# Quantised layers of a decoder block moved beside the next batch's attention, with three batches in progress

## What is computed

```python
def attention(x):                      # qkv = x @ Wqkv.T + b, one k, v of 32 columns
    scores = where(causal, q @ k.T / sqrt(32), min_val)
    return softmax(scores) @ v @ out_w.T + out_b

def smooth_quant_linear(x, w):         # twice a batch: w 512x512, then 512x256
    s = sqrt(max(amax_columns(x), EPS) / max(amax_columns(w), EPS))
    xs, ws = x / s, w * s
    x_scale, w_scale = amax_rows(xs) / 127, amax_rows(ws) / 127
    return round(xs / x_scale) @ round(ws / w_scale).T * x_scale * w_scale.T

def ffn(x):                            # DFF 1376, rank 8, 8 experts, w: top-2 weights
    gate = x @ W_gate + lora(x, sA_gate, sB_gate) + experts(x, A_gate, B_gate, w)
    up = x @ W_up + ...                # the same
    hidden = silu(gate) * up
    return hidden @ W_down + lora(hidden, ...) + experts(hidden, ...)

x = x + attention(layernorm(x))
x = x + linear(silu(gate) * up, ctx_1024)   # gate, up = linear(layernorm(x), fside)
x = x + ffn(layernorm(x))
```

## Time and profile before

| what | us |
|---|---|
| median of three runs | 1168.69 |
| lowest, highest | 1168.50, 1169.06 |
| the profiled execution | 1169.19 |
| its span, first to last instruction | 1167.1 |

### The profile page before, as it was taken

One profiled execution on the slowest core, in us unless ns is written; L12 is line 12 of the kernel. 1 busy time (PEld: TensorE's weight loads), 2 busy tenths in 40 slices (PEclk: granted clock), 3 DMA queues, 4 the chain that ended last, 5 costly groups with the idle time before them and its releaser, 6 DMA issues.

```text
span 1167.1 us, 12967 instructions
## 1 busy us (share of the span) xinstructions
PE 961.7 (82%) x5206; PEld 667.3 (57%) x5214; DVE 595.1 (51%) x801; ACT 314.3 (27%) x484; POOL 242.7 (21%) x177
## 2 busy tenths in 40 slices
PE   2698895446898998878898997878989988859997
PEld 1464353324665566656665576556655666638885
DVE  2254567654444647663644476753544566642222
ACT  2323331432132321432132313232223213311010
POOL 2412333442010214030002113220002121301010
PEclk9757686658899999998998999988999999969999
DMA  7562563526522443225325332444224422244541
GB/s 261 163 221 99 209 243 114 185 123 251 112 106 106 157 145 135 106 105 184 100 92 199 108 119 90 151 154 108 92 91 189 146 92 104 90 153 171 184 172 57
DMA packets 41439, 166.05 MB, mean 142 GB/s; under 512 B 4956, under 2 KB 7772, under 8 KB 32420
## 3 DMA queue, kind: packets, MB, share of 16 engines
q1 hardware_dynamic: 41380, 165.22, 40.8%
HBM read 120.97 MB, written 27.20 MB: 127 GB/s over the span
## 4 chain that ended last, share of the span: by engine, by line
PE 58%; DVE 24%; POOL 7%; issue 5%; ACT 3%; SPq 1%; DMA 1%; POOLq 0%; DVEq 0%; ACTq 0%
PE ring L852 8%; PE ring L853 7%; PE ring L854 7%; PE av L957 4%; DVE negm L1204 4%; PE slot L943 3%; PE den L957 3%; PE slot L923 3%; PE slot L852 3%; PE slot L853 3%; PE slot L854 3%; DVE rden L1224 3%; PE ring L1088 2%; DVE qm L1294 2%; POOL x L650 2%
## 5 line engine op out<-in xcount | busy, mean ns | idle before, releaser
L1204 DVE TENSOR_REDUCE negm<-slot 128x4 f32<-128x512 f32 (+2 forms) x96 | 99.2, 1046 | 128.7 <-PE slot L923 128.3
L852 PE MATMUL ring<-xT_h,gu 128*128 128x512 f32 x352 | 149.1, 423 | 9.8 <-DVE gated L1390 8.8
L655 POOL TENSOR_TENSOR hd_l<-hd,hd_h 128x512 fp32r<-128x512 f32 x44 | 57.4, 1305 | 463.0 <-ACT hd_h L828 463.0
L853 PE MATMUL ring<-xT_l,gu 128*128 128x512 f32 x352 | 140.9, 400 | 0.0
L854 PE MATMUL ring<-xT_h,gu 128*128 128x512 f32 x352 | 140.4, 399 | 0.0
L730 ACT ACTIVATE probs<-slot 128x256 f32<-128x256 f32 (+3 forms) x128 | 86.9, 703 | 130.0 <-PE slot L943 129.1
L852 PEld LDWEIGHTS ring<-xT_h,gu 128*128 128x128 f32 x352 | 68.4, 194 | 36.3 <-DVE gated L1390 17.4
L854 PEld LDWEIGHTS ring<-xT_h,gu 128*128 128x128 f32 x352 | 68.0, 193 | 15.7
L943 PE MATMUL slot<-qst,kst 98*128 98x128 f32 (+3 forms) x256 | 75.6, 388 | 0.0
L853 PEld LDWEIGHTS ring<-xT_l,gu 128*128 128x128 f32 x352 | 68.6, 195 | 9.9
L852 PE MATMUL ring<-dn,hd_h 128*128 128x512 f32 x176 | 74.0, 420 | 0.0
(11 more groups left out here) (194 smaller groups left out, 1741.8 us busy)
## 6 DMA issues: line engine op xcount, KB each, us to landing
gu<-gu_parts SPq DMA_DIRECT2D x44, 1280.0 KB, 5.5
dn<-dn_parts SPq DMA_DIRECT2D x8, 2304.0 KB, 8.6
gu_parts<-gu SPq DMA_DIRECT2D x11, 1280.0 KB, 5.5
qst<-qT_h SPq DMA_DIRECT2D x64, 128.0 KB, 2.4
raw_gu<-gu SPq DMA_DIRECT2D x11, 640.0 KB, 7.6
dn<-dn_parts SPq DMA_DIRECT2D x4, 1728.0 KB, 6.9
dn_parts<-dn SPq DMA_DIRECT2D x11, 576.0 KB, 6.0
x_in<-x SPq DMA_DIRECT2D x4, 1024.0 KB, 7.3
```

Of the source, the lines that this page charges most:

```text
L655: pool.tensor_tensor(hd_l[:, i, :], hd[:, :], hd_h[:, i, :].bitcast(F32), ALU.subtract).then_inc(hd_lo.sem, 1)
L852: pe.matmul(out_, w_hi_, m_hi_, start=start, stop=False, skip_group_check=True)
L853: pe.matmul(out_, w_hi_, m_lo_, start=False, stop=False, skip_group_check=True)
L1204: dve.tensor_reduce(negm[:, h0:h0 + heads, qt].rearrange("p (a c) -> p a c", a=2), slots[SLOT["max", b, g, i]][:, :, 0:heads // 2 * n].rea ...
```

## The change

Three things are done.

- **Order.** The layer has a list of its own, `layer_steps(b)`. `beside` puts it between the steps of the attention of batch b + 1, and `merged` adds the preparation's second half (b = 0) or the feed-forward of batch b - 1. The first half of the preparation stays beside the attention of batch 0. The layer of batch 3 goes with the feed-forward of batch 2; that of batch 3 still stands alone. After a step that claims a slot (`HELD`) the layer's next steps follow at once, until the slot is read.
- **Places.** `xn`, `w_raw`, `d_raw` and `wrow` exist twice: for batch 0 in the region of `xT`, from batch 1 on over the qkv weights. So these are stored once at the start (`wqkv_out`) and fetched once for batch 3 (`wqkv_again`). `hid` lies in `x_in`; `tile_max`, `rows`, `a_bf`, `th` and `x3` have a region of their own. x2 goes through memory (`x2_save`, `x2_copy`). `hd` has as many buffers as `hd_h`, and to make room there are 4 hidden slots for 5, and segments of 3, 3, 3 and 2 tiles.
- **Splits.** The statistics, norms, maxima, scalings, row maxima, the reciprocals of `context`, the bias addition and the layer's weight scaling are each issued in halves or quarters. `gated` is a step two quarters ahead of the product `hd`.

```diff
-SEGMENTS = ((0, 1, 2, 3), (4, 5, 6, 7), (8, 9, 10))
-HID_SLOTS = 5
+SEGMENTS = ((0, 1, 2), (3, 4, 5), (6, 7, 8), (9, 10))
+HID_SLOTS = 4
...
+HELD = MLP_TENANTS + ("colmax", "undo0")
...
+        yield ("turn1", b, s), 0.9, 0.3
+    if b == 0:
+        yield ("x_load", 1), 0, 0
+        yield ("x_again", 0), 0, 0
+        for tt in range(TT):
+            yield ("bias", 0, tt), 0, 0
+    yield ("kv", b), 2.8, 0.3
     for e in range(KT):
-        yield ("q", b, e), 2.2
-    yield ("v", b), 2.5
+        yield ("q", b, e), 2.8, 2.2
...
+        yield ("pause",), 0, 0.7
+        if idx in (1, 2) and g:
+            yield ("split_context", b, g - 1, idx - 1), 0, 0
...
+def layer_steps(b):
+
+
+    for h in range(2):
+        yield ("ln2_stats", b, h), 2
+    yield ("w_load", b), 0
+    for h in range(2):
+        yield ("ln2_norm", b, h), 2
     for n in range(2):
-        if n == 0:
-            yield ("ln2_stats", b), 3
-            yield ("ln2_norm", b), 4
-        else:
+        halves = range(2 - n)
+        if n:
+            yield ("d_load", b), 0
             yield ("tanh", b), 1.5
-            yield ("wmax", b, 1), 1
+        for h in halves:
+            yield ("wmax", b, n, h), 2
+        if n:
             yield ("act", b), 3
-        yield ("xmax", b, n), 3 if n == 0 else 2
-        scale = 1.0 if n == 0 else 0.6
...
+    for h in range(2):
+        yield ("residual", b, h), 2
+    yield ("x2_save", b), 0
+    yield ("x_load", b + 2), 0
+    yield ("wqkv_again", b + 2), 0
+    for h in range(2):
+        yield ("ln3_stats", b, h), 2
+    for h in range(2):
+        yield ("ln3_norm", b, h), 2
+    yield ("x_again", b + 1), 2
+    for h in range(2):
+        yield ("ln1_stats", b + 2, h), 2
+    for h in range(2):
+        yield ("bias", b + 1, 2 * h), 1
+        yield ("bias", b + 1, 2 * h + 1), 1
+        yield ("ln1_norm", b + 2, h), 1
...
+                if name == "up" and k == 1:
+                    yield ("gated", b, f), 0
...
+def beside(attention, layer, first, last):
+
+    attention, layer = list(attention), list(layer)
+    names = [step for step, _, _ in attention]
+    lo, hi = names.index(first) + 1 if first else 0, names.index(last) + 1
+    span, whole = sum(own + room for _, own, room in attention[lo:hi]), sum(w for _, w in layer)
     out, have, used, n = [], 0.0, 0.0, 0
-    for step, r in attention:
+    for i, (step, own, room) in enumerate(attention):
+        out.append((step, room))
+        if lo <= i < hi:
+            have += (own + room) * whole / span
+        while n < len(layer) and (i >= hi or i >= lo and used < have or n and layer[n - 1][0][0] in HELD):
+            used += layer[n][1]
+            out.append((layer[n][0], 0))
+            n += 1
+    return out + [(step, 0) for step, _ in layer[n:]]
+
...
+PREPARATION = list(preparation_steps())
+FIRST_PART = len(PREPARATION) // 2
+ORDER = merged([(step, room) for step, _, room in attention_steps(0)], PREPARATION[:FIRST_PART])
+ORDER += merged(beside(attention_steps(1), layer_steps(0), None, ("scores", 1, 14)), PREPARATION[FIRST_PART:])
+for _b in range(2, BATCH):
+    ORDER += merged(beside(attention_steps(_b), layer_steps(_b - 1), ("v", _b), ("scores", _b, 12)), feed_forward_steps(_b - 2))
+ORDER += merged(layer_steps(BATCH - 1), feed_forward_steps(BATCH - 2))
...
+        xn, w_raw, d_raw, wrow = ([sb(f"{name}{i}", shape, at=at) for i, at in enumerate(places)] for name, shape, places in (
+            ("xn", [P, TT, D], (xT_at, wqkv_at)), ("w_raw", [P, TT, D], (xT_at + 8192, wqkv_at + 8192)),
+            ("d_raw", [P, TT, INNER], (xT_at + 8192, wqkv_at + 8192)), ("wrow", [P, D], (a_at, wqkv_at + 16384))))
...
+            def wqkv_out():
+                sp.wait_ge(w_lo.sem, KT)
+                parts = wqkv_parts.rearrange("p i (k d) -> p i k d", k=KT)
+                sp.dma_start(parts[:, 0], wqkv_h[:, :, :].bitcast(F32)).then_inc(wqkv_stored.sem, 16)
+                sp.dma_start(parts[:, 1], wqkv_l[:, :, :].bitcast(F32)).then_inc(wqkv_stored.sem, 16)
+
+            def wqkv_again(b):
+                if 3 <= b < BATCH:
+                    sp.wait_ge(h_ready.sem, h_ready.at(b - 2, 2 * TT))
+                    parts = wqkv_parts.rearrange("p i (k d) -> p i k d", k=KT)
...
-                    sp.wait_ge(x2_ready.sem, x2_ready.at(b - 1, TT))
-                else:
-                    sp.wait_ge(x3T_ps.sem, x3T_ps.at(b - 1, KT))
+                    sp.wait_ge(o_ps.sem, o_ps.at(b - 1, 2))
...
             def x_again(b):
+                if b == BATCH:
+                    return
                 if b:
                     sp.wait_ge(xn_ready[2].sem, xn_ready[2].at(b - 1, TT))
-                    sp.wait_ge(x2_copied.sem, x2_copied.at(b - 1, 16))
+                    sp.wait_ge(x2_saved.sem, x2_saved.at(b - 1, 16))
...
             def w_load(b):
-                sp.wait_ge(t_ps.sem, t_ps.at(b, 24))
-                sp.dma_start(w_raw[:, :, :], rows_of(w[b])).then_inc(mw_loaded.sem, 16)
+                if b == 0:
+                    sp.wait_ge(wo_stored.sem, 16)
+                else:
+                    sp.wait_ge(wqkv_stored.sem, 32)
+                    sp.wait_ge(h_ready.sem, h_ready.at(b - 1, 2 * TT))
+                    if b + 1 < BATCH:
+                        sp.wait_ge(q_ps.sem, q_ps.at(b + 1, KT))
...
+            def x2_save(b):
+                sp.wait_ge(x2_ready.sem, x2_ready.at(b, TT))
+                sp.dma_start(x2_parts[b], x1[:, :, :].rearrange("p a d -> p (a d)")).then_inc(x2_saved.sem, 16)
...
+            def bias(b, tt):
+                if b == BATCH:
+                    return
+                if tt == 0:
+                    pool.wait_ge(res_loaded.sem, res_loaded.at(b, 16))
+                pool.tensor_tensor(x1[:, tt, :], x1[:, tt, :], bo_bc[:, :], ALU.add).then_inc(xb_ready.sem, 1)
...
+            def gated_(b, f):
+                dve.wait_ge(tanh_done.sem, tanh_done.at(b, f + 1))
+                dve.scalar_tensor_tensor(gated[:, :], gated[:, :], 1.0, ring[RING["gate", b, f]][:, :], ALU.add, ALU.mult)\
+                    .then_inc(gated_done.sem, 1)
...
+                n = FT * b + f - HID_SLOTS
+                if n >= 0:
+                    dve.wait_ge(out_ps.sem, TT * (segment_of(n // FT, n % FT) + 1))
```

410 lines of the change are left out of this document (217 added, 193 removed).

## The result

The changed kernel takes 1185.9 us (median of four runs, 1184.7 to 1191.1), the kernel before beside it 1168.6 (1168.1 to 1169.1). The ratio is 1.016, with a 95% interval from 1.013 to 1.019: **slower by 1.6%**, where I forecast faster by 1.9%. The range, 1108 to 1180, did not hold it either. The profiled execution took 1185.4 us, its span is 1183.6.

The account below looks back on a forecast made before the run. PE was taken as the bound, with idle time and low clock to win. Stages 184 + 180 + 243 + 243 + 159 + 137 sum to a span of 1146 us; with 1.6 us to the median, 1147, range 1108 to 1180.

Parts of the forecast that it names:

- The step that failed: Turns of batches 2 and 3: loads queued on SP behind waits of the layer cost 0, or 5 us per turn if exposed.
- Both signs: Signs that the sum is wrong: turns over 250 us, or PE waiting on gu, qst or x_in.
- rival 2: SP and POOL in order: late moves of q cost 15 us, held-up gate tiles 5 per turn, 1165 in all; chance 0.13.
- The DVE-thick stretch: Turns: DVE's first layer steps between attention's maxima, 22.9 us against 18.3 of PE's own, so about 4.5 of waiting.
- What goes: Turns: waits for hT_l, gated, the layer's chain and hd_l shrink, 12.5 us per turn in all.
- The wait for wx stays: Turns: PE's 4.8 us wait for wx remains, since its turn still stands right behind the route.
- Stage of batch 1: Attention of batch 1 beside the layer of batch 0: 165 plus 14 and 1 of waits, 180 us; ends 157 and 200.
- rival 3: DVE becomes the convoy: PE's in-order queue waits behind layer steps in merged turns and new stage, 43 us more, 1190; chance 0.14.
- First stage: Start and attention of batch 0: 178 becomes 184 us, q's first move 7 later, 1 back for half a prepared tile.
- Layer of batch 3 and tail: Layer of batch 3 beside the feed-forward of batch 2: 159 us; last feed-forward alone: 145 becomes 137.
- The clock: Stage of batch 1: the low clock is kept, about 0.65; dense work does not bring full speed back.
- rival 1: The clock comes back or the streams pack better: 23 us less, 1124, or 1114 with turns of 238; chance 0.24.

Follow-up runs that it names:

- experiment 1: Changed kernel with the load of the third gate and up tile ahead of the last q in the list: 1178.3 us; measured again for a trace, 1173.2.
- experiment 3: Changed kernel with both loads moved on SP, the third gate and up tile's ahead of the last q and the down weights' early: 1159.1 us, ratio 0.993.
- experiment 2: Changed kernel with the load of the layer's down weights moved up in the list, to behind the last read of w_raw: 1177.6 us, ratio 1.008.
- experiment 5: On experiment 3, four DVE operations in the layer's second product cut to one token tile of four, output not the reference's: 1145.5 us, ratio 0.980.
- experiment 10: On the kernel with both loads moved and four tiles prepared first, the layer's second weight maxima moved early: 1142.6 us, ratio 0.978.
- experiment 6: Kernel before with one part of the change alone, DVE's product gated behind the second tile of the up product: 1159.1 us, ratio 0.992.
- experiment 7: On experiment 3, the routing counted as 4.5 us of work in the feed-forward's list, to cover the wait for wx: 1164.0 us, ratio 0.998.
- experiment 11: On experiment 10, two weight tiles prepared in the first stage in place of four: 1134.2 us, ratio 0.970.

## Why the prediction was wrong

- **The step that failed** is in the turns: "each tile has a full tile of time (22 us) to land, so I take 0; 5 per turn if it is exposed". Measured: 8.3 us of waiting in each turn, and 10 to 12 with the longer matmuls around it; the granted clock was 0.74 in the 20 us around it, and 1.00 at that place in experiment 1, without the wait. With the down weights, an edit that I had not looked at, the two SP places are worth 27 us of the time (experiment 3). Both signs that I had named for this came: turns over 250 and PE waiting on `gu`. I had reckoned the time from a free buffer to the use, and the DMA share. Neither is the question on an in-order queue. The question is what stands ahead of the instruction on SP, and what that waits for. I named this queue in the text, and put the late moves of q at the start and the bursts behind x2_save at its risk (rival 2); the rows that cost were q's moves ahead of `gu_load`, and a `gu_load` ahead of `d_load`. The order of SP's instructions was there to be read.
- **The DVE-thick stretch**, forecast at 4.5 per turn. `negm` is up from 0.8 to 3.5, `sc` from 1.2 to 3.9, `tile_max` from 0.4 to 2.2, `cx` from 0 to 2.8 (against the turn from 520 to 771 before): 10 us. With `d_raw` early (experiments 2 and 3) 7 of them are left, so 3 hang on its load. The mechanism was right and the size half of it; the place was another: I summed the first product of the layer, and the pile is in the second, with the reciprocal of attention (1.74) and the maxima of 128x1024 (1.2 each) in it. Experiments 5 and 10 show it.
- **What goes**, forecast at 12.5 per turn: `hT_l` 6.5 and `gated` 3.8 did (experiment 6 confirms the second by itself). The 2.5 for the layer's chain and the 1 for `hd_l` did not: `a_bf` is 2.3 in place of 2.9, `hd_l` 2.0 in place of 1.6. Ten and a half in all.
- **The wait for wx stays**: 4.6, right. Why it can't be had by cover, I learned in experiment 7.
- **Stage of batch 1**: 190 for 180, within its ends of 157 and 200. My 165 was not PE's busy time: of the 121 us that I took for attention only 110.44 were busy. Read rightly, the sum was 154 busy and 26 idle; measured are 149, at a clock of 0.72 for my 0.65, and 41. So the idle time is the term that was too small. All the waits of the layer's chain came (`tile_max` 9.5, its longest 6.1), and `negm_hl` 8.3 and `negm` 9.4 on top. That is rival 3's place and mechanism: it had put 13 us over my sum there, 10 came.
- **First stage**: 170 for 184. The first move of q was at 45.65, 4 late in place of 7, and PE's wait for it grew by 3.7. The other difference is the clock, 0.84 in this execution and 0.76 before, with PE busy for 117.9 us in place of 132.3; in others of the same instructions the stage was 173 to 183 us long (see the last section). The sum flattered the change by luck here.
- **Layer of batch 3 and tail**: 156 and 135 for 159 and 137, right. PE has no wait for ln3 left there. In the first, some luck is in it: the old layer stage held 56.5 us of ring work (73.31 less 16.83), not 60, and with that my own sum gives 163.
- **The clock** did not come back in the stage of batch 1: 0.72. In experiment 11 PE was busy 18.67 of the 20 us from 60 to 80, in the attention of batch 0, at a clock of 0.62 (the row below). The forecast was right not to take rival 1. The Trainium skill's rule that work without gaps gives the full clock ("TensorE: Matmul & The Clock Gate", section "Why this matters for your kernels") is not borne out by these rows either.

```profile
60.00:80.00 20.00, 18.67 (x108) 10.74 (x111) 8.37 (x9) 6.31 (x10) 1.55 (x2) 0.62 0.27 84
```

In sum, rival 3 had the sign and nearly the time (1190), but for two thirds of the loss in the turns the wrong cause: that loss is SP's order first (32 of 46 us), DVE's convoy second.

## What to carry to other kernels

When streams are merged into one list, walk the list once for each in-order queue, SP's above all, and ask of each load what stands ahead of it and until when that waits; free buffers and free bandwidth say nothing of it. An engine that is busy for half the time can still be the bound in stretches of 15 us: look for stretches without a gap in its timeline just ahead of PE's waits, and move out of them what can be done elsewhere; filling PE's wait with other work that needs the same engine only moves it. Price small local edits apart from a large reordering: here one early operation on DVE was worth as much as the whole merge with its two loads mended, and the merge paid only when its loads, its maxima and its preparation had found their places.
